# Values projected two head pairs at a time with tokens on partitions and returned through HBM; a new order of scores and mixes

## The reference

```python
h = patch_embedding(x); h = concatenate([h, text_embedding(x_txt)])
n = layernorm(h)
q, k, v = n @ W_q, n @ W_k, n @ W_v          # 16 heads of 64
a = sigmoid(n @ W_gate + b_gate)             # per token, head and key dimension
S = a[..., None] * S + k[..., None] * v[..., None, :]    # step over the 68 tokens
o_t = einsum('bhk,bhkv->bhv', q_t, S)
h = h + out @ W_o
h = h + top2_of_8_experts(layernorm(h))      # 256 -> 512 -> 256 with relu
```

## Time and profile before

| | |
|---|---|
| median of 3 runs | 406.86 us (405.18 to 407.86) |
| profiled execution, its own time | 408.7 us |
| its span | 407.0 us |
| TensorE busy | 85% of the span |
| VectorE, ScalarE, GpSimd busy | 55%, 33%, 32% |
| mean granted TensorE clock | 0.934 |

### The profile page before, as it was taken

One profiled execution on the slowest core, in us unless ns is written; L12 is line 12 of the kernel. 1 busy time (PEld: TensorE's weight loads), 2 busy tenths in 40 slices (PEclk: granted clock), 3 DMA queues, 4 the chain that ended last, 5 costly groups with the idle time before them and its releaser, 6 DMA issues.

```text
span 407.0 us, 7752 instructions
## 1 busy us (share of the span) xinstructions
PE 344.7 (85%) x2739; PEld 299.4 (74%) x2740; DVE 222.7 (55%) x329; ACT 132.4 (33%) x279; POOL 131.1 (32%) x124
## 2 busy tenths in 40 slices
PE   4883997989989898989998999883499999999900
PEld 3663987888888888888987887573378888888800
DVE  0048799468484948577582145458235545544325
ACT  1143661444536253444344011431023223323300
POOL 5120043221312212222013699103506555554310
PEclk9997998999999999999999999966589999999965
DMA  7810011010010710000001930003102221122155
GB/s 208 289 52 2 0 53 52 4 52 2 2 53 0 317 45 0 0 0 0 1 1 26 439 159 0 0 2 110 52 26 68 66 77 65 70 70 66 41 165 202
DMA packets 10791, 28.85 MB, mean 71 GB/s; under 512 B 2000, under 2 KB 6608, under 8 KB 10128
## 3 DMA queue, kind: packets, MB, share of 16 engines
q1 hardware_dynamic: 8336, 21.99, 14.9%
q0 software_dynamic: 2432, 6.56, 5.6%
HBM read 23.17 MB, written 5.37 MB: 70 GB/s over the span
## 4 chain that ended last, share of the span: by engine, by line
PE 64%; DVE 9%; issue 9%; POOL 8%; DMA 7%; ACT 1%; SPq 1%; DVEq 0%; POOLq 0%; ACTq 0%
PE ps L716 10%; PE ps L381 8%; PE ps L503 7%; PE ps L382 7%; PE ps L383 7%; PE ps L518 5%; POOL w1lo L1415 5%; DVE U L1048 4%; PE ps L488 4%; PE ps L695 3%; PE ps L697 3%; PE ps L696 3%; PE ps L706 2%; POOL w1hi L1413 2%; DMA pt<-patches 2%
## 5 line engine op out<-in xcount | busy, mean ns | idle before, releaser
L381 PE MATMUL ps<-xnhi,wlo 128*128 128x272 f32 x256 | 77.4, 302 | 16.1 <-DVE kU L1054 9.0
L382 PE MATMUL ps<-xnlo,whi 128*128 128x272 f32 x256 | 75.5, 295 | 0.0
L383 PE MATMUL ps<-xnhi,whi 128*128 128x272 f32 x256 | 75.2, 294 | 0.0
L381 PEld LDWEIGHTS ps<-xnhi,wlo 128*128 128x128 f32 x256 | 49.9, 195 | 19.2 <-DVE kU L1054 10.4
L1062 DVE RECIPROCAL invU<-U 128x272 f32<-128x272 f32 x32 | 56.7, 1813 | 0.0
L943 ACT ACTIVATE hr<-ps,b 128x128 f32<-128x128 f32 x96 | 27.4, 367 | 81.3 <-PE ps L706 81.3
L1367 POOL TENSOR_TENSOR qA<-qraw,invU 128x544 f32<-128x544 f32 x16 | 22.3, 1392 | 95.3 <-DVE invU L1062 75.5
L382 PEld LDWEIGHTS ps<-xnlo,whi 128*128 128x128 f32 x256 | 49.8, 195 | 0.0
L383 PEld LDWEIGHTS ps<-xnhi,whi 128*128 128x128 f32 x256 | 49.7, 194 | 0.0
L1048 DVE TENSOR_TENSOR_SCAN U<-u_g,first 128x544 f32<-128x544 f32 x16 | 29.8, 1865 | 28.9 <-ACT u_g L827 28.9
L716 PE MATMUL ps<-w,hr 128*128 x192 | 45.2, 379 | 0.0
(11 more groups left out here) (166 smaller groups left out, 526.3 us busy)
## 6 DMA issues: line engine op xcount, KB each, us to landing
wraw<-w_attn SPq DMA_DIRECT2D x8, 512.5 KB, 3.4
w<-w SPq DMA_DIRECT2D x1, 4096.0 KB, 15.2
w<-w SPq DMA_DIRECT2D x1, 3072.0 KB, 10.6
yin<-yrows SPq DMA_DIRECT2D x4, 384.0 KB, 4.5
wo<-w_o SPq DMA_DIRECT2D x1, 1024.0 KB, 14.0
w<-w SPq DMA_DIRECT2D x1, 1024.0 KB, 5.9
b<-b SPq DMA_DIRECT2D x1, 1024.0 KB, 17.1
xrows<-xrow SPq DMA_DIRECT2D x2, 512.0 KB, 3.0
```

The costliest lines, as they stand in the source:

```text
L381: pe.matmul(dst, slo, mhi[n], start=(i == 0), stop=False)
L382: pe.matmul(dst, shi, mlo[n], start=False, stop=False)
L383: last = pe.matmul(dst, shi, mhi[n], start=False, stop=(i == len(pairs) - 1))
```

## The change

The four projections of a pair become three (`MATS` = 3). Values are computed for two pairs at once: a tile of 128 tokens of the stream is the stationary operand, and 256 columns of `W_v` (`wv`, split into `wvhi` and `wvlo`) are the moving one, six matmuls for each of nine tiles, so tokens come out on partitions. Two tiles make a piece (five pieces, the last with one tile of 64 tokens), a piece fills bank 6. ScalarE copies it to a staging tile `vst`, SyncE writes it to an HBM tensor `vrows`, and reads each pair's values from there into `vb` in the layout by batch. Pieces of pairs 0 and 1 stand in the first projections, those of pairs 2 and 3 in pair 1, of 4 and 5 in pair 2, of 6 and 7 in pair 4; pairs 3, 5, 6 and 7 have none. `turn_values`, `vT` and `e_g` are gone. The scores of a group alternate between the heads. The mix of group 3 of pair hp-2 now stands behind the first gate projection of pair hp. The 3 MB of expert weights are loaded in six parts, one in each of the pairs 1 to 6.

```diff
+            def value_tiles(j, bank):
+
+                for q in range(2 if j < VC - 1 else 1):
+                    r = 2 * j + q
+                    w = P if r < VT - 1 else VTAIL
+                    tok = slice(r * P, r * P + w)
+                    dst = ps[0:w, bank, q * VW:(q + 1) * VW]
+                    for m in range(DC):
+                        pe.matmul(dst, xnlo[:, m, tok], wvhi[:, m, :], start=(m == 0), stop=False)
+                        pe.matmul(dst, xnhi[:, m, tok], wvlo[:, m, :], start=False, stop=False)
+                        last = pe.matmul(dst, xnhi[:, m, tok], wvhi[:, m, :], start=False, stop=(m == DC - 1))
+                last.then_inc(s_vmm, 1)
+
+            def values(k, j):
+
+                pe.wait_ge(s_wvlo, k + 1)
+                pe.wait_ge(s_vev, VC * k + j)
+                value_tiles(j, 6)
...
+            def pair_step(hp, par, k, chunks, loaded):
+
+                def chunk(at):
+                    if at in chunks:
+                        values(k, chunks[at])
+
+                pe.wait_ge(s_wlo, hp + 1)
+                if early(hp, 2):
+                    pe.wait_ge(s_exp, 2)
+                    pe.wait_ge(s_ku, 2)
+                pe.wait_ge(s_qraw, 2 * hp - 1)
+                project(hp, par, GATE, 0)
+                if not early(hp, 2):
+                    mix(hp - 2, par, G - 1, loaded[par])
+                pe.wait_ge(s_qraw, 2 * hp)
+                project(hp, par, GATE, 1)
+                if early(hp, 2):
+                    pe.wait_ge(s_vev, VC)
+                pair_scores(hp - 1, 1 - par, 0)
+                pe.wait_ge(s_exp, 2 * hp + 1)
+                project(hp, par, KEY, 0)
+                chunk(1)
+                pe.wait_ge(s_exp, 2 * hp + 2)
+                project(hp, par, KEY, 1)
+                mix(hp - 1, 1 - par, 0, loaded[1 - par])
+                chunk(2)
+                pair_scores(hp - 1, 1 - par, 1)
+                pe.wait_ge(s_ku, 2 * hp + 1)
+                project(hp, par, QUERY, 0)
+                chunk(3)
+                mix(hp - 1, 1 - par, 1, loaded[1 - par])
+                pair_scores(hp - 1, 1 - par, 2)
+                chunk(4)
+                pe.wait_ge(s_ku, 2 * hp + 2)
+                project(hp, par, QUERY, 1)
+                mix(hp - 1, 1 - par, 2, loaded[1 - par])
+                pair_scores(hp - 1, 1 - par, 3)
+                chunk(5)
 
...
-                    pe.wait_ge(s_vt, 2 * HP)
-                elif not (early(a, 1) and g == 0):
-                    pe.wait_ge(s_p, 4 * a + g)
-                for h in range(2):
-                    rows = slice(DK * h, DK * (h + 1))
-                    for b in range(GB):
-                        t = slice((GB * g + b) * T, (GB * g + b + 1) * T)
+                    for h in range(2):
+                        rows = slice(DK * h, DK * (h + 1))
                         last = pe.matmul(ps[0:T, bank + h, b * T:(b + 1) * T], kU[par][rows, t], qA[par][rows, t],
                                          start=True, stop=True)
                 last.then_inc(s_pmm, 1)
 
...
+            def store_values(k, j):
+
+                sp.wait_ge(s_vev, VC * k + j + 1)
+                at = 2 * j * P
+                if j < VC - 1:
+                    sp.dma_start(vrows[k, at:at + 2 * P].rearrange("(q p) d -> p q d", p=P), vst[j % 2][:]
+                                 ).then_inc(s_vst[j % 2], 16)
+                else:
+                    sp.dma_start(vrows[k, at:TOK], vst[j % 2][0:VTAIL, 0]).then_inc(s_vst[j % 2], 16)
+
+            def load_values(hp):
+
+                for i in range(2):
...
-
-            sp.dma_start(w1[:, 0:EARLY_W], w_1[:, 0:EARLY_W]).then_inc(s_w1, 16)
-            sp.dma_start(b1[:], b_1).then_inc(s_bias, 16)
+                    sp.wait_ge(s_omm, 4 * (hp - 1))
+                c = (hp % 2) * P
+                sp.dma_start(vb[hp % 2][0:T], vrows[hp // 2, :, c:c + P].rearrange("(b t) d -> t b d", t=T)
+                             ).then_inc(s_vb[hp % 2], 16)
...
+            def load_value_weights(k):
+
+                sp.wait_ge(s_wvlo, k)
+                sp.dma_start(wv[:], w_v[k]).then_inc(s_wv, 16)
+
+            load_value_weights(1)
+            for j in range(VC):
+                store_values(0, j)
+            load_values(0)
+            load_values(1)
+            for hp in range(1, HP):
+                if hp + 1 < HP:
+                    sp.wait_ge(s_wlo, hp)
+                    sp.dma_start(wraw[(hp + 1) % 2][:], w_attn[hp + 1, :, 0:WA + 1]).then_inc(s_wload[(hp + 1) % 2], 16)
+                k = hp // 2 + 1
+                if k < IT:
+                    for j in (range(VC) if hp == 1 or hp % 2 == 0 else ()):
+                        store_values(k, j)
+                if hp % 2 and k + 1 < IT:
+                    load_value_weights(k + 1)
+                if hp >= 2:
+                    load_values(hp)
+                if hp <= EARLY_W:
+                    sp.dma_start(w1[:, hp - 1], w_1[:, hp - 1]).then_inc(s_w1, 16)
+
             sp.wait_ge(s_ok, 1)
             in_range = sp.value_load(ok_sum[0:1, 0:1], min_val=0, max_val=P)
             with sp.If(in_range < P):
...
+            def split_values(k):
+
+                act.wait_ge(s_wv, 16 * k + 16)
+                if not early(k, 1):
+                    act.wait_ge(s_vmm, VC * k)
+                act.activation(wvhi[:], wv[:], ACT.Copy).then_inc(s_wvhi, 1)
+
...
+            def pair_step(hp, par, k, chunks, wload, tail=False):
+
+                def chunk(at):
+                    if at in chunks:
+                        evacuate_values(k, chunks[at])
+
                 evacuate_gate(hp, par, 0)
-                if early(hp, 2):
-                    evacuate_v(0, 0, 1)
+                if not early(hp, 2):
+                    evacuate_o(hp - 2, G - 1)
                 evacuate_gate(hp, par, 1)
-                if early(hp, 2):
-                    evacuate_v(0, 0, 2)
-                    evacuate_v(0, 0, 3)
                 if not tail:
                     split_pair(hp + 1, 1 - par, wload)
+                chunk(1)
+                evacuate_o(hp - 1, 0)
+                chunk(2)
                 evacuate_q(hp, 0)
+                chunk(3)
+                evacuate_o(hp - 1, 1)
+                chunk(4)
                 evacuate_q(hp, 1)
-                evacuate_vt(hp, 0)
-                evacuate_vt(hp, 1)
-                for g in range(G):
-                    evacuate_v(hp, par, g)
-                    evacuate_o(hp - 1, g)
+                evacuate_o(hp - 1, 2)
+                chunk(5)
 
             act.wait_ge(s_const, 4)
...
             def pair_step(hp, par):
-                decay(hp, par)
+                scan(hp, 0)
                 mask(hp - 1, 0)
-                for g in range(3):
-                    invert(hp, g)
+                scan(hp, 1)
+                decay_keys(hp, par, 0)
+                decay_keys(hp, par, 1)
+                in_bounds(hp)
+                invert(hp, 0)
                 mask(hp - 1, 1)
+                invert(hp, 1)
                 mask(hp - 1, 2)
+                invert(hp, 2)
                 invert(hp, 3)
                 mask(hp - 1, 3)
 
...
+            def split_values(k):
+
+                pool.wait_ge(s_wvhi, k + 1)
+                pool.tensor_tensor(wvlo[:], wv[:], wvhi[:].bitcast(F32), ALU.subtract).then_inc(s_wvlo, 1)
+
             split_pair(0, 0)
             pool.memset(u_g[:].rearrange("p (b t) -> p b t", t=T)[:, :, 0:1], 0.0).then_inc(s_first, 1)
+            split_values(0)
             split_pair(1, 1)
             scale_q(0, 0)
+            split_values(1)
             pair_step(1, 1)
-            with pool.Fori(2, HP - 2, 2) as i:
-                pair_step(i, 0)
-                pair_step(i + 1, 1)
+            with pool.Fori(1, IT - 1) as it:
+                split_values(it + 1)
```

More of the change, by code:

```diff
@@ L56 @@
 LN_EPS = 1e-5
-MATS = 4
-GATE, KEY, QUERY, VALUE = range(MATS)
+MATS = 3
+GATE, KEY, QUERY = range(MATS)
 WA = MATS * DC * P
+WG = WA + 1 + DC * P
+VW = 2 * P
+WV = DC * VW
+VT = -(-TOK // P)
+VC = -(-VT // 2)
+VTAIL = TOK - (VT - 1) * P
+IT = HP // 2
 WF = DC * FH
@@ L162, in build @@
         wlo = [sb(f"wlo{i}", [P, MATS, DC, P], F32R) for i in range(2)]
+        wv = sb("wv", [P, DC, VW])
+        wvhi = sb("wvhi", [P, DC, VW], F32R)
+        wvlo = sb("wvlo", [P, DC, VW], F32R)
+        vst = [sb(f"vst{i}", [P, 2, VW]) for i in range(2)]
         attn_end = cursor[0]
@@ L332, in _ @@
-            sp.dma_start(b1[:], b_1).then_inc(s_bias, 16)
+            for hp in range(2):
+                sp.dma_start(wraw[hp][:], w_attn[hp, :, 0:WA + 1]).then_inc(s_wload[hp], 16)
+                if hp == 0:
+                    sp.dma_start(wv[:], w_v[0]).then_inc(s_wv, 16)
+            sp.dma_start(wo[:], w_o).then_inc(s_wo, 16)
+            sp.dma_start(wg[:], w_gate).then_inc(s_wg, 16)
+            sp.dma_start(b1[:], b_1).then_inc(s_bias, 16)
+            def store_values(k, j):
```

(24 more changed lines are left out.)

180 lines of the change are left out of this document (90 added, 90 removed).

## The result

The changed kernel takes 416.05 us (median of 4 runs, 412.22 to 417.73), the kernel before 406.02 us beside it (403.61 to 407.86). The ratio is 1.024, with a 95% interval of 1.014 to 1.034: 10 us slower, where 21 us faster was forecast. The profiled execution took 412.22 us, with a span of 410.5; it is the fastest of the four.

What follows compares the result with a forecast made beforehand. TensorE's list was taken as the bound, VectorE's chain behind it. Walking the pairs gained 23 us, less 2 for late transfers: 21 us from 408.7 is 387.7, or 386 on the median's scale; range 379 to 397.

Steps and rivals of the forecast that it cites:

- The walk over the pairs: Attention, pair by pair from first gate projections: pair 6's last mix at 190.8 where it stood at 213.86, 23 us gained.
- Values through HBM: Reads of `vb` for pairs 3 and 5: hidden to 4 us late; 2 us allowed with weight transfers, ends 0 and 9.
- Rival 4: HBM reads and the one queue make transfers late, landings about 12 us: 25 us, 411 us; chance 0.07, weak or full.
- The scores: Score groups with alternating heads: 0.63 for 0.94, by the mix; 0.3 less a group, 1.25 us a pair.
- Rival 1: The scores of the two heads don't overlap, each group 0.31 more: 8 us, 394 us; chance 0.14.
- VectorE's loop: From mask through mix, gate projection, scan and back to mask: 15.9 us for a pair without pieces after another such.
- Rival 2: VectorE's second scan still meets GpSimd's `wlo`, 1.4 us in pairs 3, 5, 6: 5 us, 391 us; chance 0.12.
- Pieces: Five pieces of values bring TensorE's sum to 21.4 us in a pair; forecast 23.1 in pair 2, 22.2 in pair 4.
- Rival 5: A piece might cost 0.19 for each matmul if the weight load bounds it; chance 0.07 together with other waits.
- the late `wv`: Pair 2: `wv` requested behind pair 1's last store, ScalarE's gate exp 3 us late, K0 waits 1.7 us.
- `wvlo` in pair 1: First piece waits 3.0 us for GpSimd's `wvlo`; slower matmuls at the lower clock after it cost 1.4 us more.
- The clock: TensorE's clock falls after gaps in pairs bound by VectorE: about 10 us, 396 us; chance 0.08.

Runs made afterwards that it cites:

- the requests ahead: On the kernel with the read as 64 and 4 partitions, `wraw` asked for one pair earlier, `wv` before the stores, `wvlo` before pair 0's `qA`: 382.43 us.

## Why the prediction was wrong

The walk over the pairs, against the traces of the changed kernel and of the one with the read as 64 and 4 partitions (us from one first gate projection to the next; pair 7 is counted to the start of pair 6's last mix). Both are profiled executions; that of the changed kernel is 3.8 us under its median, which the walk doesn't explain.

| | forecast | changed kernel | with the cut at 64 |
|---|---|---|---|
| pair 1 | 25.2 | 37.0 | 27.6 |
| pair 2 | 23.1 | 22.4 | 23.4 |
| pair 3 | 15.2 | 23.1 | 15.8 |
| pair 4 | 22.2 | 22.1 | 22.1 |
| pair 5 | 15.2 | 22.4 | 16.9 |
| pair 6 | 15.9 | 15.7 | 15.7 |
| pair 7 to the mix | 18.2 | 18.0 | 18.0 |
| together | 135.0 | 160.7 | 139.4 |

- **The step that failed** is "Values through HBM": for a read of 544 KB a bound of 6.7 us, the time of a 256 KB read the earlier trace rows, and 2 us allowed for all late transfers, 9 at most. Alone, a read took about 10 us, and 12.2 with others behind it. The nearest rows all had 128 partitions outermost, and a weight load of the kernel before reached a share of 0.88 of the DMA engines; this read has 68 partitions and a share of 0.28. Pairs 1, 3 and 5 took 11.8, 7.9 and 7.2 us more than forecast, 26.9 together. With the read at 16 engines they take 22.2 us less, and the whole kernel 24 us less (392.24 against 416.05), or 24.5 (382.43 against 406.93). The mixes waited for reads of `vb`, which the prediction had named as a sign that it is wrong. The trace of before couldn't show the slow read, but the shape was in the diff, and the prediction named its bytes and runs and not its partitions.
- **What is left** with the read wide is 4.4 us over the walk, and the kernel then stands at 0.970 of the time before where 0.949 was forecast. 2.4 of the 4.4 lie in pair 1 (`wraw` and `wvlo`) and 1.7 in pair 5, where a mix waits 1.7 us for ScalarE's `oT`, which stands behind ScalarE's wait of 5.9 us for `wraw`. Besides these, pair 1 starts 1.3 us later than forecast there and the tail takes 1.5 us longer than before. So the allowance of 2 us for late transfers was too small even with all engines.
- **Rival 4** named this mechanism, with 14 us for its worst landing, 411 us for its time and 0.07 for its chance. Its time was 5 us off, in part by luck, since its reason was not the one found: it took the reads to be slow behind others, and judged that from a crowded start. It named `wv` of pair 2 and the weights of pairs 4 and 6; the largest single stall was `wraw` of pair 2, which the forecast had among the transfers under the 2 us.
- **The scores** went to 0.64 as the mix row said, not to 0.94 and not to the 0.47 of an ideal pair of row tiles. Rival 1 was wrong here; its price of 8 us was near the 5.5 to 6.8 measured.
- **VectorE's loop** of 15.9 us for a pair without pieces held within 0.2 (15.7, and 15.85 between mixes with the read wide). The second scan took 1.29, not 2.70: it begins at 188.47 and `wlo` at 189.34, as walked. Rival 2 was wrong.
- **Pieces** in the even pairs came out right (22.4 and 22.1 for 23.1 and 22.2). Rival 5 was wrong. In pair 2 the late `wv` cost 0.7 rather than 1.7; ScalarE's gate exp began 2.7 us late there rather than 3, which is the smaller part of that.
- **`wvlo` in pair 1** held TensorE 4.0 us for 3.0, with matmuls of 0.21 us behind it as forecast, and went with the order changed.
- **The clock** was priced only as a rival, for gaps in pairs that VectorE bounds. Those kept 1.00. It fell after the waits of 3.96, 8.51, 5.60 and 5.09 us, and in the tail, where the forecast left everything as before: from pair 6's last mix to the end of the attention before took 7.3 us and now about 9.7. In another execution the tail kept its clock, so this is not bound to the change.

With the read wide and the requests ahead the time is 0.946 of the time before, against the forecast's 0.949. That is no confirmation of the sum: the requests ahead took away 4.4 us for `wvlo` and 1.7 for `wv` that the forecast had charged.

## What to carry to other kernels

A DMA is priced by bytes, by the length of its runs and by the size of its outermost dimension: 68 partitions moved at 66 GB/s where 64 and 4 moved at up to 276, and a read took 10 us in place of 5. Where one engine issues all transfers, a slow one delays all that follow, and an engine that waits in order passes that on, so a wait is traced back through the queue (mix, bank, ScalarE's list, weights, SyncE, the read) before its price is set. A walk along the waits with durations from rows held to within a microsecond in pairs 2, 4, 6 and 7, and failed where a transfer was priced from rows of another shape.

## What the runs showed of the hardware

- A read of `vb` on few engines stretches SyncE's next request: 5.75 and 7.88 us on the queue behind it where 0.43 is usual. With the read as 64 and 4 partitions the request of `wraw` in pair 1 took 0.46 us, and with 34 and 34 it took 6.96.
- Eight products that alternate between the lower and the upper 64 partitions take 0.64 us, where four of one half and then four of the other take 0.94.
- VectorE's scan and GpSimd's product of two SBUF tensors hold each other up by who begins: where the scan began at 188.47 and took 1.29, `wlo` from 189.34 took 2.05 in place of 1.82, and where `wvlo` ran from 140.75 for 1.29, the scan that began at 141.58 took 1.60.
- The tail of the attention, after the same wait of 2.07 us and with the same groups, ran at a granted clock of 0.50 in one execution (mixes of 1.1 us) and of 1.00 in another (0.63 us).
